# VectorE's attention program without its loop, and another order of the opening, in a gated cross-attention and expert kernel

## The reference

```
def attn(xn, ctx, Wq, Wk, Wv, Wo, bo):            # 16 heads of 16
    scores = (xn @ Wq.T) . (ctx @ Wk.T) * 0.25    # by head
    scores = where(tril(512 x 1601), scores, -inf)
    return softmax(scores) @ (ctx @ Wv.T) @ Wo.T + bo
def ffn(x, gate_w, w_gate, w_up, w_down):         # 8 experts, each takes 128 tokens of a batch
    gating, idx = top_k(softmax(x @ gate_w.T).T, 128)
    h = silu(x[idx] @ w_gate.T) * (x[idx] @ w_up.T)
    return zeros.at[idx].add(gating * (h @ w_down.T))
x = x + tanh(g_xattn) * attn(layernorm(x), ctx, ...)
x = x + tanh(g_ffn) * ffn(layernorm(x), ...)
```

## Time and profile before

| what | us |
|---|---|
| median of 3 runs (lowest, highest) | 1915.38 (1913.03, 1917.52) |
| profiled execution | 1915.71 |
| its span, first to last instruction | 1913.9 |
| TensorE busy | 1782.3 (93%) |
| VectorE busy | 1055.4 (55%) |
| ScalarE busy | 928.1 (48%) |
| GpSimd busy | 929.5 (49%) |
| attention, first max matmul to the end of the pipeline | 53 to about 830 |
| experts, loads of the first weights to the end | 855 to 1914 |

### The profile page before, as it was taken

The page is one execution under the profiler, slowest core; times in us unless marked ns, Lnnn a source line. Parts: engine busy times, 40 slices in busy tenths (PEclk is TensorE's granted clock), DMA queues, the critical chain, the costliest instruction groups (busy, mean ns, idle before and its releaser), DMA issues.

```text
span 1913.9 us, 41403 instructions
## 1 busy us (share of the span) xinstructions
PE 1782.3 (93%) x13414; PEld 1051.3 (55%) x13414; DVE 1055.4 (55%) x2649; ACT 928.1 (48%) x1812; POOL 929.5 (49%) x1028
## 2 busy tenths in 40 slices
PE   3799999999999999954899999999999999999997
PEld 1455555555555555521456566565656565656565
DVE  2677777777777777737643434434334434343431
ACT  2366666666666666633343334434333434343332
POOL 4467777777777777444234242423232423333322
PEclk9899999999999999977999999999999999999999
DMA  6767777777777777438464664545636545455221
GB/s 149 170 167 167 186 186 187 185 186 185 185 188 185 187 186 167 116 95 213 89 115 83 129 116 85 102 84 106 129 62 129 103 86 100 89 92 84 49 34 23
DMA packets 411290, 247.70 MB, mean 129 GB/s; under 512 B 293271, under 2 KB 392735, under 8 KB 411167
## 3 DMA queue, kind: packets, MB, share of 16 engines
q1 hardware_dynamic: 386591, 212.53, 47.7%
q0 software_dynamic: 24576, 33.57, 10.8%
HBM read 118.63 MB, written 58.72 MB: 93 GB/s over the span
## 4 chain that ended last, share of the span: by engine, by line
PE 50%; DVE 2%; SPq 1%; DMA 1%; POOL 1%; ACT 0%; issue 0%; POOLq 0%
PE bank L1099 11%; PE bank L1101 11%; PE bank L1100 11%; PE bank L1116 6%; PE bank L1117 6%; PE bank L1115 6%; SPq L1026 1%; DMA gate_raw<-in_L_ffn_w_gate 1%; DVE h L1217 0%; DVE h L1220 0%; ACT h L1145 0%; SPq L1005 0%; DVE top_at L1167 0%; POOL gate_nat L1044 0%; POOL up_nat L1044 0%
## 5 line engine op out<-in xcount | busy, mean ns | idle before, releaser
L1065 POOL DMA_INDIRECT out<-y,row_now x128 | 201.8, 1577 | 604.9 <-ACT y L1152 579.9
L583 ACT ACTIVATE prob<-bank 128x512 f32<-128x512 f32 x640 | 365.6, 596 | 168.6 <-PE bank L476 100.1
L1217 DVE TENSOR_TENSOR h<-bank,silu 128x512 f32<-128x512 f32 x256 | 176.4, 689 | 395.2 <-PE bank L1101 269.5
L1145 ACT ACTIVATE h<-h 128x512 bf16<-128x512 f32 x256 | 161.1, 629 | 347.2 <-DVE h L1217 347.2
L673 DVE CUSTOM_DVE_ANT_0 masked<-bank,causal 128x384 bf16<-128x384 f32 (+1 forms) x512 | 299.8, 617 | 52.7 <-PE bank L453 50.3
L453 PE MATMUL bank<-ks,qs 96*128 96x128 bf16 (+3 forms) x1024 | 276.6, 306 | 21.9 <-DMA ks<-k_parts 12.5
L1115 PE MATMUL bank<-downT,h 128*128 128x256 bf16 x1024 | 279.1, 273 | 0.0
L1116 PE MATMUL bank<-downT,h 128*128 128x256 bf16 x1024 | 279.1, 273 | 0.0
L1117 PE MATMUL bank<-downT,h 128*128 128x256 bf16 x1024 | 279.1, 273 | 0.0
L1220 DVE TENSOR_TENSOR h<-h 128x512 bf16<-128x512 f32 x256 | 177.2, 692 | 179.4 <-ACT h L1145 179.4
L1099 PE MATMUL bank<-tokT,gateT 128*128 128x512 bf16 x512 | 194.8, 381 | 33.7 <-DMA tokT<-rows 28.9
(11 more groups left out here) (147 smaller groups left out, 2920.0 us busy)
## 6 DMA issues: line engine op xcount, KB each, us to landing
q_parts<-q_sb SPq DMA_DIRECT2D x64, 192.0 KB, 2.9
k_parts<-k_sb SPq DMA_DIRECT2D x64, 192.0 KB, 3.5
qs<-q_parts SPq DMA_DIRECT2D x64, 192.0 KB, 3.0
ks<-k_parts SPq DMA_DIRECT2D x64, 192.0 KB, 3.2
x_t<-in_x SPq DMA_DIRECT2D x16, 512.0 KB, 3.9
ctx_t<-in_ctx SPq DMA_DIRECT2D x16, 512.0 KB, 4.9
qs<-q_parts SPq DMA_DIRECT2D x64, 128.0 KB, 2.9
ks<-k_parts SPq DMA_DIRECT2D x64, 128.0 KB, 3.2
```

What stands on the lines that cost most here:

```text
L583: nc.scalar.activation(prob[:, gr % 2, h0:h0 + nh, POFF[tiles[0]]:POFF[tiles[0]] + w], sc_bank[SC_BANK[k]][:, 0:nh * w].rearrange("p (h w) ...
L1065: nc.gpsimd.indirect_dma_start(out_rows, bass.IndirectOffsetOnAxis(ap=row_now[:, par, c, s:s + 1], axis=0), y[:, c % 2, s, :], None, compu ...
```

## The change

It touches `attention` alone. VectorE gets `rounds_apart`, which emits all rounds from -1 to 17 as straight-line code; the other four engines keep the loop. In the opening, SP loads x and ctx ahead of all weights; the gates and the bias are issued by ScalarE; ScalarE makes `xn` of batch 0 before it copies the weights; GpSimd builds the mask rows' tiles before batch 0's power and shift, and they are 512 columns wide (`NT` = 4 times 128), so that the DMAs that spread them write rows of 1 KB, 16 per partition, instead of 256 bytes, 64 per partition. These two DMAs are issued behind `kstack` of batch 0, group 1, instead of ahead of the rounds. GpSimd waits for the bias in batch 0's "res" instead of ahead of its rounds.

```diff
-    tail_of = {n: sb(ctx, f"{n}_tail", [P, P], BF16) for n in ("q", "k")}
+    tail_of = {n: sb(ctx, f"{n}_tail", [P, NT, P], BF16) for n in ("q", "k")}
...
+    def rounds_apart(body):
+
+        for b in range(-1, BATCH + 2):
+            for p in steps(b):
+                body(b, p)
+
...
+                    if n == "k" and gr == 1 and isinstance(b, int) and b == 0:
+                        sp.wait_ge(tails_made, 6)
+                        for tail, full, first in (("q", qs, ROWS), ("k", ks, STACK)):
+                            dst = full[first:P, :, :, :].rearrange("p g h t -> p (g h) t")
+                            sp.dma_start(dst, tail_of[tail][first:P, :, :].rearrange("p j c -> p (j c)").unsqueeze(1)
+                                         .broadcast_to([P - first, GROUPS * GH, T])).then_inc(tails, 16)
...
-            load_weights("wq")
             load(0)
-            for n in ("wk", "wv", "wo"):
+            for n in ("wq", "wk", "wv", "wo"):
                 load_weights(n)
             sp.dma_start(gw_raw[:, :], g["gate_w"]).then_inc(w_loaded["gate_w"], 16)
-            sp.dma_start(bo_rep[:, :], g["bo"].partition_broadcast(P)).then_inc(gates_loaded, 16)
-            sp.dma_start(gates[:, 0:1], g["g_xattn"].partition_broadcast(P)).then_inc(gates_loaded, 16)
-            sp.dma_start(gates[:, 1:2], g["g_ffn"].partition_broadcast(P)).then_inc(gates_loaded, 16)
-            sp.wait_ge(tails_made, 6)
-            for n, to, first in (("q", qs, ROWS), ("k", ks, STACK)):
-                dst = to[first:P, :, :, :].rearrange("p g h (j c) -> p (g h j) c", c=P)
-                sp.dma_start(dst, tail_of[n][first:P, :].unsqueeze(1).broadcast_to(
-                    [P - first, GROUPS * GH * NT, P])).then_inc(tails, 16)
             rounds(sp, piece)
...
+            act.dma_start(gates[:, 0:1], g["g_xattn"].partition_broadcast(P)).then_inc(gates_loaded, 16)
+            act.dma_start(gates[:, 1:2], g["g_ffn"].partition_broadcast(P)).then_inc(gates_loaded, 16)
+            act.dma_start(bo_rep[:, :], g["bo"].partition_broadcast(P)).then_inc(gates_loaded, 16)
+            act.wait_ge(gates_loaded, 48)
+            nc.scalar.activation(tanh_g[:, :], gates[:, :], ACT.Tanh).then_inc(tanh_done, 1)
+            piece(-1, ("ln1+", 0, 0))
+            piece(-1, ("ln1+", 0, 1))
+            for n, (name, o) in enumerate(order):
...
+            def later(body, p):
+                if p[0] == "ln1+" and isinstance(p[1], int) and p[1] == 0:
+                    return
+                piece(body, p)
+
+            rounds(act, later)
...
-            rounds(dve, piece)
+
+            rounds_apart(piece)
...
                     wait(pool, res_loaded, count(b, 16, 16))
+                    if isinstance(b, int) and b == 0:
+                        pool.wait_ge(bias_done, 1)
...
             pool.wait_ge(consts, CONSTS)
-            piece(-1, ("ln1", 0, 1))
-            nc.gpsimd.memset(tail_of["q"][:, :], 1.0).then_inc(tails_made, 1)
+            nc.gpsimd.memset(tail_of["q"][:, :, :], 1.0).then_inc(tails_made, 1)
...
-            pool.wait_ge(bias_done, 1)
+            piece(-1, ("ln1", 0, 1))
             rounds(pool, piece)
```

More of the change, by code:

```diff
@@ L553, in _ @@
         def _(act):
[L554 to L567, removed]
             def piece(body, p):
@@ L637, in piece @@
                     nc.scalar.activation(lexp[:, :, :], logit[:, :, :], ACT.Exp).then_inc(lexp_done, 1)
-            rounds(act, piece)
+            act.dma_start(gates[:, 0:1], g["g_xattn"].partition_broadcast(P)).then_inc(gates_loaded, 16)
[6 more added lines that the diff above has]
+            for n, (name, o) in enumerate(order):
+                act.wait_ge(turned, n + 1)
+                for i in range(NH2):
+                    dst, src = turned_weights(name, o, i, 0, job_bank[n % 2])
+                    last = nc.scalar.activation(dst, src, ACT.Copy)
+                last.then_inc(hi_taken, 1)
+            n = len(order)
+            act.wait_ge(turned, n + 1)
+            act.wait_ge(evac, n)
+            nc.scalar.activation(gwT[:, :, 0:EXPERTS], job_bank[n % 2][:, 0:NH2 * EXPERTS].rearrange(
+                "p (i c) -> p i c", i=NH2), ACT.Copy).then_inc(evac, 1)
+            def later(body, p):
[3 more added lines that the diff above has]
+            rounds(act, later)
         @block.vector
@@ L854, in _ @@
             pool.wait_ge(consts, CONSTS)
[L855 to L857 removed]
+            nc.gpsimd.memset(tail_of["q"][:, :, :], 1.0).then_inc(tails_made, 1)
+            nc.gpsimd.memset(tail_of["k"][:, :, :], 0.0).then_inc(tails_made, 1)
             pool.wait_ge(tails_made, 2)
[L859 to L860 removed]
+            nc.gpsimd.affine_select(out=tail_of["k"][:, :, :], in_=tail_of["k"][:, :, :], compare_op=ALU.is_ge, fill=NEG,
+                                    base=-1 - SUB * (STACK + 1), pattern=[[0, NT], [-1, P]], channel_multiplier=SUB)\
                 .then_inc(tails_made, 1)
[L862 to L863 removed]
+            nc.gpsimd.affine_select(out=tail_of["q"][:, :, :], in_=tail_of["q"][:, :, :], compare_op=ALU.is_ge, fill=0.0,
+                                    base=SUB * ROWS, pattern=[[0, NT], [1, P]], channel_multiplier=-SUB)\
                 .then_inc(tails_made, 1)
             pool.wait_ge(tails_made, 4)
[L866 removed]
+            nc.gpsimd.memset(tail_of["k"][STACK:ROWS, :, :], 1.0).then_inc(tails_made, 1)
             pool.wait_ge(tails_made, 5)
[L868 to L869 removed]
+            nc.gpsimd.affine_select(out=tail_of["q"][:, :, :], in_=tail_of["q"][:, :, :], compare_op=ALU.is_ge, fill=0.0,
+                                    base=-1 - SUB * (STACK + 1), pattern=[[0, NT], [-1, P]], channel_multiplier=SUB)\
                 .then_inc(tails_made, 1)
[L871 removed]
+            piece(-1, ("ln1", 0, 1))
             rounds(pool, piece)
```

3 lines of the change are left out of this document (removed).

## The result

The changed kernel runs 1911.85 us in the median (1908.62 to 1912.59), the kernel before 1915.98 us beside it (1913.03 to 1918.89), 14 runs of each. The ratio is 0.9972, with a 95% interval of 0.9965 to 0.998: 0.28% faster, 4.1 us. The forecast was 11.1 us. The direction was right; the size was not, and the time lies 0.85 us above the range.

A forecast was written before the change was run, and what follows sets the result against it. Attention was taken as bound by TensorE's matmuls, leaving only idle time to gain: -8.2 (opening) + 0.5 (mask rows) - 3.4 (loop) = -11.1 us, from 1915.4 to a median of 1904.3 us; range 1899 to 1911.

The forecast's parts named there:

- Items 1 and 2: Opening: xn made ahead of the weights' copies, the weights then decide; first projection at 20.4 instead of 28.65, minus 8.2 us.
- Rival E: Opening: something unseen, such as late gates or slow GpSimd, holds it; half the gain, 1908.5 us; chance 0.07.
- Item 4: Attention loop: VectorE without a loop saves 0.31 us in each of 11 batches, 3.4 us, bounds 0 to 4.9.
- Rival B: Attention loop: the other four engines' register work keeps TensorE at 48.15 us a batch; 1907.7 us; chance 0.11.
- D: Whole kernel: more than forecast, all 4.9 of the loop, no collision, better clock; 1900.7 us; chance 0.08.
- The price of the fetches: Attention: fetching VectorE's instructions for 11 more batches costs nothing, covered by VectorE's idling some 10 of 48 us.
- rival C: Attention: VectorE's straight-line code stalls on instruction fetches; slower, 1928.7 us at 1.5 us a fetch; chance 0.05.
- Item 3: Batch 0: mask rows' DMAs, 3.2 us of traffic against 2.5 of slack before batch 1's transposed x; +0.5, bounds 0 to 4.3.
- rival A: First batch: mask rows keep their old rate and hold it up, costing 4.3 us; 1908.1 us; chance 0.11.
- Item 6: First batch: TensorE's granted clock pattern moves along with the opening; plus or minus 1.6 us, taken at 0.
- it moves as a whole: Experts' part: not touched by the diff, so it only shifts in time; no term in the sum.

The follow-up runs named there:

- the repeat of after: The changed kernel run and profiled once more, nothing altered: 1060.8 us from the gating turn to the end, 2.52 us of waiting for batch 1's transposed x.
- the loop alone: The kernel before with only VectorE's rounds written out as straight-line code: 1910.96 us, ratio 0.9978.
- the mask rows early: The changed kernel with the two mask-row DMAs put back ahead of SyncE's rounds: 1904.27 us, ratio 0.9939.
- the two repeats of before: The unchanged kernel before, profiled again; from the gating turn to the end 1059.2 and 1058.8 us.
- the two kernels without the collision: The changed kernel with the mask-row DMAs ahead of SP's rounds, or behind batch 0's transposes: 1904.27 and 1904.88 us.

## Why the prediction was right or wrong

**Items 1 and 2, the opening: right.** -8.1 instead of -8.2, and some -9.5 in the repeat of after (first attention matmul at 44.01, against 53.4 to 53.8 in before's three profiles). The shift was ready at 10.19 (9.99 + 0.20; forecast 10.0), xn started at 10.22, the projection at 20.56 (forecast 20.4), released by the last weights' copy, as said; the first attention matmul came at 45.24 (forecast 45.2). Rival E is out: its sign, a projection after 22, isn't there.

**Item 4, VectorE's loop: right in size and in mechanism.** -3.3 in the two profiles and -3.2 with the loop alone, against -3.4. The signs were less exact. VectorE's time from one remainder to the next (line 705 after, 691 before), at 393.29 and 396.41, is 3.12 us, not 3.0, where the loop had 3.21:

```profile
393.29 0.69 DVE L705 TENSOR_TENSOR rest<-bank,q_sb 128x512 f32<-128x512 f32 x1 [0.68 <-ACT q_sb L597]
...
396.41 0.68 DVE L705 TENSOR_TENSOR rest<-bank,q_sb 128x512 f32<-128x512 f32 x1
```

And TensorE's 0.22 us for the maxima shrank to 0.18 and didn't vanish. That row shows only a part of the wait: in the loop alone, 0.24 of the 0.33 us an iteration are weight loads that wait less for VectorE's maxima, as the prediction said, and 0.09 one that waits less for its remainder of k, which it didn't name. Rival B is out, and so is D, which wanted 4.9. The price of the fetches, nothing, is right: q14 carried 13 packets from 232 to 708 us, and VectorE's idle time named "issue" there is 0.2 us in all, so rival C is out. (Its price was also added up unevenly: 21 us less the whole forecast of 11.1 would have been 1925.3, not 1928.7.)

```profile
q14 instruction: 13, 0.11, 0.1%
```

**Item 3, the mask rows: this is the step that failed.** It took +0.5 from bounds of 0 and 4.3; the pair of profiles shows +4.8, the means of all profiles +5.7, and the place of the two DMAs alone is worth 7.6 us between medians (1911.85 - 1904.27, in different sets of runs; by the ratios, 0.33% or 6.3 us). Its parts:

- The traffic was sized at 3.2 us, with the rate of rows of 1 KB in the opening. Those go to 128 partitions, at 41 ns a packet (0.894 x 6 us x 16 / 2083); the mask rows go to 30 and 32 partitions and take 95. With that, 992 packets take 5.9 us. The row that the estimate should have gone by stood beside it: the mask rows' own window, 6.8 us, and its partitions were named in rival A as the reason for doubt.
- Against the 2.5 us of slack, which was right, stand in after 0.9 us by which the first transpose is issued later than 8.1 us ahead of its old time (47.29 instead of 46.4), and the landing of the last one 12.3 us behind that issue (the second is issued at 52.6 and lands 7.0 later) instead of 6.0 (60.5 - 54.5). 0.9 + 6.3 - 2.5 = 4.7, the wait in the profile. The 6.3 are about the mask rows' 5.9. That SP's issue is slow with them ahead (8.51 us for two transposes) I read as the same traffic, seen from the issuing side, since the sum closes without it; no run separates the two.
- "In the slack of a batch that idles 6.2 us anyhow": that idle time lies elsewhere in the batch. The wait for xT is paid in full, and the time at the lower clock that it brings is paid on top.

**Rival A is what happened**, with its mechanism (the partitions more than the packets' size set the rate) and its sign (a wait for batch 1's transposed x above 1 us). Its price of 4.3 fits the wait (2.5 to 4.7); the clock, which it left out, makes it 4.8 in this pair and 5.7 on the means. It was given 0.11. The page of the Trainium skill named there ("DMA: Bandwidth & Descriptors", Why small descriptors are slow) was cited for an estimate by which the widening gives only a fifth; the landings in the late place, 8.0 against 9.8 us, agree with that, and the traffic itself gained less, 5.9 against 6.8 us.

**Item 6, the clock**, was taken at 0 with 1.6 to either side. With the mask rows early, the stretch from the first attention matmul to batch 1's copy took 52.35 us (44.65 to 97.0) instead of 53.3; but the two repeats of before took 52.4 and 52.3, so this is scatter and no gain. With them late, and a stop from 55 to 60 us, the clock was at 0.50 until 63.0 instead of 55.7. What this costs isn't a term of its own but a supplement to a wait in that place.

**What no step had: the experts' part**, "it moves as a whole". It took 2.3 us more on the means of the profiles (1061.1 against 1058.8). Rival A's own forecast of 1908.1 misses by 3.7 us for this and for the clock behind the wait.

**The sum, as it came out**: -8.1 + 4.8 - 3.3 + 2.9 = -3.7 in the first pair of profiles. On the means of the two profiles of after and the three of before it is -8.9 + 5.7 - 2.8 + 2.2 = -3.8, and the medians have -4.1, instead of -11.1. With the rows early the medians have -11.1, which looks like the forecast and is partly luck: the two kernels without the collision have on the means of their profiles -8.7 for the opening, -3.6 for the loop, +2.4 for the experts and nothing else, -9.9 in all, where their medians have -11.1 and -10.5. About 1 us between profiles and medians isn't located.

## What to carry to other kernels

Price a DMA that is moved by the rows of a transfer of its own shape, on the same partitions, and not by that of a transfer with the same packet size; then set it against the slack of whatever is queued behind it, and count a wait there in full, and more than in full where TensorE's clock is still low (5.7 us for waits of 2.5 to 4.7). A bulk fill with constants, which nothing needs soon, belongs where its queue has nothing else that is urgent: here ahead of SP's rounds or behind batch 0's transposes, both of which beat the kernel before and the changed one (1904.27 and 1904.88 us against 1915.35 and 1911.85). Where a loop's engines sit at 98% of the bound, writing one engine's program out can still be worth 0.3 us an iteration; measure that edit alone, since its gain is easily hidden by what is changed with it, and look for it in the waits of the weight loads as well as of the matmuls. Profile the unchanged kernel more than once before reading a difference of 1 us in one stretch.

## What the runs showed of the hardware

- A packet of 1 KB within SBUF took 46 to 48 ns with 128 partitions, 79 to 86 with 64, 81 with 32, and 95 for the mask rows on 30 and 32. The 64 and 32 were always the upper ones. Repeating a source row made no difference with 128. Packets of 256 bytes on 30 and 32 partitions took 27 ns (0.522 x 13 us x 16 / 3999): 6.8 us for all mask rows against some 5.9 in rows of four times the width.
- SP's issue of two transposes took 8.51 us with the mask rows queued ahead of them and 2.65 without.
- TensorE's granted clock stayed at 0.50 until 63.0 us in a stretch in which it stood still for 4.70 us, and rose at 55.7 us in one in which it worked on. Behind the turn of the experts' loop, the 20 us had a mean of 0.91 in some programs and 0.83 in others, which was worth about 1.0 us.
- VectorE's attention program of all batches in a row, without a loop, showed no stop for instructions: 13 packets in 476 us.
- Four weight loads of TensorE in each iteration waited 0.33 us less in all for VectorE once VectorE's program had no loop.
- The experts' part, whose source is the same in all kernels, took 1058.4 to 1059.2 us in one group of programs and 1060.7 to 1061.5 in the other. Why its loop's turn is longer there is open.
